# First layer's expert rows scattered to token order; the second convolution loads them plainly

## The reference

```
x = x + relu(segment_sum(Z[src] * edge_weight))         # Z = layernorm(x) @ W
x = x + ffn0(layernorm(x))      # attention (8 heads), then 64 experts, top 2
x = x + conv1(layernorm(x))     # mean of neighbours @ W_l.T + x @ W_r.T, relu, batch norm
x = x + ffn1(layernorm(x))      # 8 experts, top 2, hidden 256
```

```
pos  = place of the choice in its expert's queue        # cumulative count
keep = pos < C                                          # the rest is dropped
buf  = zeros(E, C, H).at[ef, posc].add(tok)             # 64 x 78 rows of 512
h    = gelu(buf @ w1[e] + b1[e]);  y = h @ w2[e] + b2[e]
out  = sum over the 2 choices of y[ef, posc] * (gate * keep)
```

## Time and profile before

| what | value |
|---|---|
| median of three runs | 1474.98 us (1473.58 to 1478.74) |
| the profiled execution: its own time | 1486.91 us |
| its span, first to last instruction | 1485.1 us |
| mean granted TensorE clock | 0.974 |
| TensorE matmuls busy | 1405.3 us, 95% |
| VectorE / ScalarE / GpSimd busy | 750.1 / 464.1 / 225.5 us |
| first experts, first turn to last output product | 782.61 to 1052.45 us |
| from there to the first neighbour sum | to 1103.65 us |
| DMA moved | 142.38 MB |

### The profile page before, as it was taken

The page is one execution under the profiler, slowest core; times in us unless marked ns, Lnnn a source line. Parts: engine busy times, 40 slices in busy tenths (PEclk is TensorE's granted clock), DMA queues, the critical chain, the costliest instruction groups (busy, mean ns, idle before and its releaser), DMA issues. The chain is left out here.

```text
span 1485.1 us, 24276 instructions
## 1 busy us (share of the span) xinstructions
PE 1405.3 (95%) x7939; PEld 904.7 (61%) x7940; DVE 750.1 (51%) x1591; ACT 464.1 (31%) x1153; POOL 225.5 (15%) x356
## 2 busy tenths in 40 slices
PE   8999999999999999999988999999899999889968
PEld 4688854455477777776556666666445555646632
DVE  7899956552278788875662222222250012544421
ACT  3599931111055555553021111111340011211111
POOL 1133310000000000000212222222420000012234
PEclk9999999999999999999998999999999999799988
DMA  5000000020000000001338999999420000823336
GB/s 153 29 0 0 0 0 0 0 85 0 28 2 2 1 2 1 2 1 48 113 72 271 322 332 322 328 323 324 138 60 0 0 0 0 301 53 128 127 95 171
DMA packets 94075, 142.38 MB, mean 96 GB/s; under 512 B 13301, under 2 KB 50571, under 8 KB 93879
## 3 DMA queue, kind: packets, MB, share of 16 engines
q1 hardware_dynamic: 69313, 97.52, 21.4%
q0 software_dynamic: 14976, 26.81, 6.5%
q10 hardware_dynamic: 9718, 17.12, 3.4%
HBM read 115.09 MB, written 26.29 MB: 95 GB/s over the span
## 5 line engine op out<-in xcount | busy, mean ns | idle before, releaser
L1240 PEld LDWEIGHTS ps<-b_r 128*128 128x128 f32 x1024 | 125.4, 193 | 34.3 <-issue 32.8
L1240 PE MATMUL ps<-b_r 128*128 128x78 f32 x1024 | 123.2, 274 | 1.1 <-DVE b_r L1302 1.1
L1249 PE MATMUL ps<-b_r 128*78 128x512 f32 x256 | 122.0, 600 | 0.0
L585 PE MATMUL ps<-b_r 125*125 125x160 f32 x660 | 118.3, 315 | 0.0
L500 ACT ACTIVATE b_r<-b_r 125x125 f32<-125x125 f32 x330 | 107.6, 389 | 9.2 <-DVE b_r L395 4.8
L1286 ACT ACTIVATE b_r<-ps,b_r 128x78 f32<-128x78 f32 x128 | 34.7, 323 | 230.5 <-PE ps L1240 226.7
L911 PEld LDWEIGHTS ps<-b_r 125*64 125x64 f32 x1600 | 85.3, 136 | 24.6 <-issue 22.8
L874 PE MATMUL ps<-b_r 64*125 64x417 f32 (+1 forms) x480 | 95.3, 529 | 1.4 <-DVE ps L1003 1.2
L911 PE MATMUL ps<-b_r 125*64 125x125 f32 x1600 | 94.7, 272 | 1.3 <-ACT b_r L939 1.3
L1144 POOL TENSOR_TENSOR b_x<-b_x,b_r 125x512 f32<-125x512 f32 x10 | 12.7, 1273 | 534.7 <-DVE b_r L1089 534.7
L1165 POOL DMA_INDIRECT b_r<-rows,b_ex_ids x88 | 85.7, 974 | 45.8 <-issue 40.7
(11 more groups left out here) (262 smaller groups left out, 2238.5 us busy)
## 6 DMA issues: line engine op xcount, KB each, us to landing
b_r<-L_ffn_w SPq DMA_DIRECT2D x128, 512.0 KB, 9.5
y<-b_r ACTq DMA_DIRECT2D x64, 156.0 KB
b_r<-L_ffn_W SPq DMA_DIRECT2D x2, 4096.0 KB, 20.5
y<-b_r ACTq DMA_DIRECT2D x24, 256.0 KB, 2.4
rows<-b_r SPq DMA_DIRECT2D x2, 2400.0 KB
b_x<-x SPq DMA_DIRECT2D x5, 480.0 KB
out<-b_x SPq DMA_DIRECT2D x10, 240.0 KB
y<-b_r SPq DMA_DIRECT2D x1, 2048.0 KB, 11.0
```

The source lines that it names most:

```text
L585: last = pe.matmul(T.ps[:P, 2 + b, 0:WC], T.weighted[:, b, j, :], T.cells[:, b, j, :], start=(j == 0), stop=(j == CJ - 1))
L1240: last = pe.matmul(T.ps[:, 2 + r % 2, f * CAP:(f + 1) * CAP], T.ew1[r % WS][:, k, f * 128:(f + 1) * 128], T.ex_t[:, r % 2, k, :], start=(k ...
L1249: last = pe.matmul(T.ps[:CAP, 4 + r % 2, :], T.eh[:, r % 2, f, :], T.ew2[r % WS][:, f, :], start=(f == 0), stop=(f == FK - 1))
```

## The change

1. `y0` has 2 * 1250 rows, in token order: row j * 1250 + token holds the expert output of choice j. In the attention block SyncE writes x into all of it once (4 DMAs, 5.1 MB), so that rows of dropped choices hold finite numbers.
2. The table gives 4128 for an empty place (iota with offsets, `EMPTY` added). A second table `sids` (10 more matmuls, `make_choices`, and two more VectorE operations) gives j * 1250 + token. Indirect DMAs get a bound and leave out indices beyond it; in the second layer's gathers too.
3. `first_experts`: 4 slots for gathered and for output rows; GpSimd issues the gathers straight from `ids` as written out, and the stores as indirect DMAs (scatters) six experts behind. ScalarE stores nothing.
4. After the last expert, in the same block: the 32 weight transposes and their copies, then the 10 products gates @ b2 with VectorE adding them to x; SyncE waits for the last scatter and loads `y0` with 20 plain DMAs (10 of 120 partitions and 2 tiles, 10 of 5 partitions), on one semaphore for each pair of tiles.
5. `second_convolution` has no gathers, no weight turns and no bias product; its filler matmuls stay.
6. `finish` waits on one semaphore for each pair of tiles (4 gathers) where it waited for 2 gathers of a tile. Several semaphores are shared; that changes no order.

```diff
 def token_ids(dve, link, T, bank, rows, columns):
-    link(dve.tensor_copy(T.ids_low[:rows, 0:columns], T.ps[:rows, bank, 0:columns]))
+    link(dve.tensor_scalar(T.ids_low[:rows, 0:columns], T.ps[:rows, bank, 0:columns], float(EMPTY), None, ALU.add))
     dve.scalar_tensor_tensor(out=T.ids[:rows, 0:columns], in0=T.ps[:rows, bank, columns:2 * columns], scalar=float(P),
                              in1=T.ids_low[:rows, 0:columns], op0=ALU.mult, op1=ALU.add)
+    link(dve.scalar_tensor_tensor(out=T.ids_low[:rows, 0:columns], in0=T.ps[:rows, bank, columns:2 * columns],
+                                  scalar=float(P), in1=T.ids_low[:rows, 0:columns], op0=ALU.mult, op1=ALU.add))
+def choice_ids(dve, T, bank, rows, columns):
+    return dve.scalar_tensor_tensor(out=T.sids[:rows, 0:columns], in0=T.ps[:rows, bank, 0:columns],
+                                    scalar=float(N), in1=T.ids_low[:rows, 0:columns], op0=ALU.mult, op1=ALU.add)
@@ attention, sync
+            for j in range(TOP):
+                for p0, p1 in ((0, 120), (120, P)):
+                    sp.dma_start(A.y0[j * N:(j + 1) * N].rearrange("(t p) d -> p t d", t=NT)[p0:p1], T.x[p0:p1])\
+                      .then_inc(S.rows_filled, 16)
+            sp.wait_ge(S.rows_filled, 80)
@@ gather_rows
         pool.indirect_dma_start(slots[:parts, r % 2, :], None, rows,
-                                bass.IndirectOffsetOnAxis(ap=T.ex_ids[:parts, r % 4:r % 4 + 1], axis=0))\
+                                bass.IndirectOffsetOnAxis(ap=T.ex_ids[:parts, r % 4:r % 4 + 1], axis=0),
+                                bounds_check=N - 1, oob_is_err=False)\
@@ first_experts
+    PEEL, SLOTS, LAG = 4, 4, 6
-            for slot in range(2):
+            for slot in range(SLOTS):
                 sp.wait_ge(S.ex_loaded[slot], 16)
             for slot in range(EARLY, WS):
                 load_expert(sp, T, S, A, slot, slot)
...
+            for slot in range(SLOTS):
+                sp.wait_ge(S.ey_stored[slot], 16 * E0 // SLOTS)
+            for i in range(NT // 2):
+                for p0, p1 in ((0, 120), (120, P)):
+                    for j, rows in enumerate((T.rows_a, T.rows_c)):
+                        sp.dma_start(rows[p0:p1, 2 * i:2 * i + 2],
+                                     A.y0[j * N:(j + 1) * N].rearrange("(t p) d -> p t d", t=NT)[p0:p1, 2 * i:2 * i + 2])\
+                          .then_inc(S.y_gathered[i], 16)
         def _(pool):
-            gather_rows(pool, T, A.rows0, T.ex, CAP, E0 // 4 - 2, S.ex_ids_ready, S.ex_turned, S.ex_loaded)
+            def gather(e):
+                if e >= SLOTS:
+                    pool.wait_ge(S.ex_turned, e - SLOTS + 1)
+                pool.indirect_dma_start(T.ex[:CAP, e % SLOTS, :], None, A.rows0,
+                                        bass.IndirectOffsetOnAxis(ap=T.ids[:CAP, e:e + 1], axis=0),
+                                        bounds_check=N - 1, oob_is_err=False).then_inc(S.ex_loaded[e % SLOTS], 16)
+            def scatter(e):
+                pool.wait_ge(S.ey_copied, e + 1)
+                pool.indirect_dma_start(A.y0, bass.IndirectOffsetOnAxis(ap=T.sids[:CAP, e:e + 1], axis=0),
+                                        T.ey[:CAP, e % SLOTS, :], None,
+                                        bounds_check=TOP * N - 1, oob_is_err=False).then_inc(S.ey_stored[e % SLOTS], 16)
+            for e in range(E0 + LAG):
+                if e < E0:
+                    gather(e)
+                if e == LAG:
+                    pool.wait_ge(S.rows_filled, 80)
+                if e >= LAG:
+                    scatter(e - LAG)
@@ tensor, after the last output product
+            for i, w in enumerate((T.w_a, T.w_b)):
+                for k in range(KD):
+                    bank = banks[KD * i + k]
+                    if bank >= 4 and i > 0:
+                        pe.wait_ge(S.ey_copied, E0)
+                    for m in range(KD):
+                        last = pe.transpose(T.ps[:, bank, m * 128:(m + 1) * 128], w[:, m, k * 128:(k + 1) * 128], T.ident[:])
+                    last.then_inc(S.wl_turned, 1)
+            pe.wait_ge(S.b2_loaded, 16)
+            pe.wait_ge(S.wl_copied, 2)
+            for t in range(NT):
+                if t >= 2:
+                    pe.wait_ge(S.bias_added, t - 1)
+                pe.matmul(T.ps[:P, 6 + t % 2, :], T.gates_t[:, t * P:(t + 1) * P], T.b2_rows, start=True, stop=True)\
+                  .then_inc(S.bias_done, 1)
@@ second_convolution, tensor
-            pe.wait_ge(S.wl_loaded, 32)
-            for i, w in enumerate((T.w_a, T.w_b)):
...
-            pe.wait_ge(S.wl_copied, 2 * KD)
-            pe.wait_ge(S.b2_loaded, 16)
...
-                pe.wait_ge(S.y_gathered[t], 32)
-                gated_sum(pe, T, t, t % 2, T.gates_t, T.b2_rows, rows).then_inc(S.moe_done, 1)
+                pe.wait_ge(S.y_gathered[t // 2], 64)
+                for j in range(TOP):
+                    last = pe.matmul(T.ps[:P, t % 2, :], T.diagonal[:, t % 2, j, :], rows[j][:, t, :],
+                                     start=(j == 0), stop=(j == TOP - 1))
@@ finish
-                pe.wait_ge(S.y_gathered[t], 64)
+                pe.wait_ge(S.y1_gathered[t // 2], 64)
```

More of the change, by code:

```diff
@@ L705, in make_table, with make_choices @@
     return last
+def make_choices(pe, T, bank, rows, place, columns):
+    for t in range(NT):
+        last = pe.matmul(T.ps[:rows, bank, 0:columns], T.place_rows[:, t * TOP + 1, :], place[:, 1, t, 0:columns],
+                         start=(t == 0), stop=(t == NT - 1))
+    return last
 def token_ids(dve, link, T, bank, rows, columns):
-    link(dve.tensor_copy(T.ids_low[:rows, 0:columns], T.ps[:rows, bank, 0:columns]))
+    link(dve.tensor_scalar(T.ids_low[:rows, 0:columns], T.ps[:rows, bank, 0:columns], float(EMPTY), None, ALU.add))
     dve.scalar_tensor_tensor(out=T.ids[:rows, 0:columns], in0=T.ps[:rows, bank, columns:2 * columns], scalar=float(P),
                              in1=T.ids_low[:rows, 0:columns], op0=ALU.mult, op1=ALU.add)
+    link(dve.scalar_tensor_tensor(out=T.ids_low[:rows, 0:columns], in0=T.ps[:rows, bank, columns:2 * columns],
[3 more added lines that the diff above has]
+                                    scalar=float(N), in1=T.ids_low[:rows, 0:columns], op0=ALU.mult, op1=ALU.add)
 def load_expert(sp, T, S, A, e, slot):
@@ L1185, in first_experts @@
     FK = F0 // 128
-    LOOPS = (E0 - 2) // WS
+    PEEL, SLOTS, LAG = 4, 4, 6
+    LOOPS = (E0 - PEEL) // WS
     def experts(engine, step):
-        for r in range(2):
+        for r in range(PEEL):
             step(0, r)
         with engine.Fori(0, LOOPS) as q:
-            for r in range(2, 2 + WS):
+            for r in range(PEEL, PEEL + WS):
                 step(q, r)
-        for r in range(2, 2 + (E0 - 2) % WS):
+        for r in range(PEEL, PEEL + (E0 - PEEL) % WS):
             step(LOOPS, r)
@@ L1267, in _ @@
             output(LOOPS, (E0 - 1) - WS * LOOPS)
+            banks = (6, 7, 0, 1, 2, 3, 4, 5)
+            pe.wait_ge(S.wl_loaded, 32)
+            pe.wait_ge(S.eh_ready, E0)
+            for i, w in enumerate((T.w_a, T.w_b)):
[8 more added lines that the diff above has]
+            pe.wait_ge(S.wl_copied, 2)
+            for t in range(NT):
+                if t >= 2:
+                    pe.wait_ge(S.bias_added, t - 1)
+                pe.matmul(T.ps[:P, 6 + t % 2, :], T.gates_t[:, t * P:(t + 1) * P], T.b2_rows, start=True, stop=True)\
+                  .then_inc(S.bias_done, 1)
         @block.scalar
@@ L1288, in step @@
                 last.then_inc(S.eh_ready, 1)
-                if not isinstance(q, int) or WS * q + r > 0:
-                    store(q, r - 1)
             experts(act, step)
-            store(LOOPS, (E0 - 1) - WS * LOOPS)
-            for slot in range(2):
-                act.wait_ge(S.ey_stored[slot], 8 * E0)
+            banks = (6, 7, 0, 1, 2, 3, 4, 5)
+            for i in range(2):
+                for k in range(KD):
+                    act.wait_ge(S.wl_turned, KD * i + k + 1)
+                    act.activation(T.wl_t[:, i, k, :], T.ps[:, banks[KD * i + k], :], ACT.Copy).then_inc(S.wl_copied, 1)
         @block.vector
@@ L1318, in _ @@
             output(LOOPS, (E0 - 1) - WS * LOOPS)
+            for t in range(NT):
+                dve.wait_ge(S.bias_done, t + 1)
+                dve.tensor_tensor(T.x[:, t, :], T.ps[:P, 6 + t % 2, :], T.x[:, t, :], ALU.add).then_inc(S.bias_added, 1)
 def second_convolution(nc, T, S, A):
@@ L1328, in second_convolution @@
     with nc.Block() as block:
[L1330 to L1336, removed]
         @block.tensor
@@ L1402, in counts @@
                 act.activation(T.ct_f[:, t], T.ct[:, t], ACT.Copy).then_inc(S.ct_ready, 1)
-            for i in range(2):
-                for k in range(KD):
-                    act.wait_ge(S.wl_turned, 4 * i + k + 1)
-                    act.activation(T.wl_t[:, i, k, :], T.ps[:, 4 * i + k, :], ACT.Copy).then_inc(S.wl_copied, 1)
             for t in range(2):
```

(1 more changed line is left out.)

94 lines of the change are left out of this document (46 added, 48 removed).

## The result

| | median us | runs | ratio to the kernel before, 95% |
|---|---|---|---|
| before | 1475.13 | 1473.58 to 1478.74 | |
| after | 1460.64 | 1455.69 to 1462.1 | 0.9891 [0.9864, 0.9919] |

The change gains 14.5 us in this comparison (medians of four runs each; the 1474.98 that the forecast starts from is the median of three); two later ones of the same two kernels gave 19.7 (ratio 0.987 [0.985, 0.9891]) and 19.1 us (0.9877 [0.9851, 0.9904]). Forecast were 22.8 us and 1452, with a range of 1444 to 1469. The profiled execution of the changed kernel took 1460.3 us, span 1458.5.

What follows compares the result with a forecast made beforehand. The expert stage was taken as bound by the latency of a two-deep gather, hardly by TensorE. Terms -4.9 - 17.4 - 1.5 + 1.0 = -22.8 us took the 1474.98 median to 1452.2, 1452 for short; range 1444 to 1469.

Steps and rivals of the forecast that it cites:

- The start (-4.9): First experts: four early gathers end TensorE's 2.9 us wait, output product at full clock takes 1.88 us: gain 4.9 us.
- The pace (-17.4): Expert stage, 63 remaining output products: 3.80 us each after, 4.08 before: gain 17.4 us (13.6 to 21.8).
- The sign that GpSimd's queue moves about 8 MB each way: Expert stage, expected in the profile after: GpSimd's queue at about 8 MB each way, DMA still at 300 GB/s or more.
- Why 4.0 before: Expert stage before: gather landing 6.8 us after issue, two slots, loop of 8.1 us for two steps, 4.05 each.
- Empty places: Rival, expert stage: empty places still cost a transfer, pace stays about 4.05 us, total 1467.9 us; chance 0.17.
- The seam (-1.5): Last output product to neighbour sums: first gated product 4.5 us later, ten tiles faster, sum -1.5 us (-4 to +6).
- The rival of the held SyncE: Seam: full queues hold SyncE's load issues, block ends 7.4 us later, total 1459.6 us; chance 0.13.
- finish (+1.0): Last block: tile 0 waits for four gathers, first product 2.8 us later; taken as +1.0 us (-1.5 to +3).
- The 4 us to be had back at tiles 8 and 9: End of finish: with a later start these tiles may avoid a wait and half clock, up to 4 us back.
- The base: Whole kernel: profiled execution 11.9 us above the median; difference carried over to the median, 1474.98 - 22.8 = 1452.2 us.
- GpSimd: Rival, expert steps: GpSimd becomes the bound; gain gone at 2.6 us a scatter, about 1532 us at 3.5; chance 0.08.

Runs made afterwards that it cites:

- the kernel with two lists: Changed kernel with 8 of the 20 loads left in SyncE's expert-stage list and 12 issued at the second convolution's start: 1452.63 us, ratio 0.9852.

## Why the prediction was right, and where it was off

Right in direction and place, and in half of the cause; 8.3 us too much in this comparison, 3 to 4 in the other two. By the means of three profiles each, the difference is 22.6 us: -0.8 to F, -24.9 in F to E, +1.3 in E to N, +0.8 in N to G, +1.0 behind it. That this meets the 22.8 of the forecast is luck: F to E gained 2.6 more than its two terms and E to N 2.8 less, and the three profiled executions of before (1480.8 in the mean) lie above its medians of 1475.1 to 1477.6. What the change is worth is the medians' 14.5 to 19.7.

- **The start (-4.9).** From F to the start of the third output product: 19.6, 17.3 and 19.4 us before, 15.9, 15.9 and 13.5 after, so -3.7 in the mean. The four early gathers did away with the wait of 2.9 us. The rest of the term was a product at the full clock, 1.88 us, and in two of three profiles it ran at the low level (3.57 and 3.52 us; in the first the granted clock is 0.66 over 785 to 790). In the third it took 1.88, and the gain was there.
- **The pace (-17.4).** Too cautious: 3.73 in all three profiles where I took 3.80. The mis-sized part is the price of a MB of weights. Over 800 to 1000 us their queue took 86.0% of 200 us for 56.55 MB, 3.04 us a MB or 3.19 an expert and not 3.42, and gathers and scatters 0.42. That is 3.61 us an expert, under TensorE's 3.73. Before, the same window has 3.24 us a MB (80.3% for 49.54 MB), and with all rows gathered 3.34: the price is higher where the share is above 1, so one read under overload was too dear for a kernel with fewer bytes. (The sign that GpSimd's queue moves about 8 MB each way was a slip: 64 times my 0.062 MB is 4 each way.) So the 61 steps gained 20 to 23 us.
- **Why 4.0 before.** I named the latency of a two-deep gather. That is half of it. With two slots and fewer bytes the pace is 3.75, with four slots and all bytes 3.73 until the stock of weights is gone. In these kernels the loop of two slots binds only where the DMA engines are overloaded: over 800 to 1000 us the share is 1.05 before and 1.06 with two slots and all rows, both with waits for gathers, and 0.94 with two slots alone, where one turn waits 0.5 us.
- **Empty places.** The rival fell. Gathering all rows put 6.27 MB back on GpSimd's queue (24.46 and not 18.19); 3068 empty places of 2 KB are 6.28. Its page has:

```profile
q0 software_dynamic: 14592, 24.46, 5.8%
```

- **The seam (-1.5).** This failed: +1.3 in the mean and +3.7 against the second profile of before. Three terms: SyncE's list took 13.25 us and not 8.8, ending 3.9 late; the fillers took 5.04 and not 4.1, as TensorE had idled 5.2 us first; the tiles and what follows them took 29.9 us and not 31.1. Of that, VectorE's first add to its last took 22.9 us (2.54 a tile in the mean; most steps are 2.39, three are 1.7, 3.0 and 3.8), as forecast with 2.5; but before it had taken 28.8 (3.2 a tile), not nine times 2.97, so the nine tiles saved 5.9 and not 4.2, and tile 0 saved 1.3 of its 1.8. The rival of the held SyncE was half right: the mechanism holds and was put at 0.13, with 3.9 of its 7.4 us. My argument against it, issues into empty queues, was true for the first fourteen loads only (0.30 to 0.45 us each; the last six take 0.38 to 2.23, 7.4 in all).
- **finish (+1.0).** As forecast in the main: the first product 2.3 us later behind G (2.8 foreseen), and two tiles at the low clock ahead of eight without a wait. The 4 us to be had back at tiles 8 and 9 were there in the first profile of before only; the other two have no such wait.
- **The base.** I carried 11.9 us of the profiled execution over to the median, and said that the gain shrinks by what of it is gather waiting: that was 5.3. With it the pace's gain is that of the typical execution, F to E 264.6 to 242.4, -22.2, where the two terms said -22.3. What is then missing of 22.8 is the seam, and some 2 to 3 us spread over stretches that the change doesn't touch (to F: 777.7 to 782.8 among all profiles; N to G: 330.9 to 335.4).
- **GpSimd.** Never near the bound: 1.02 and 0.97 us. Beside VectorE's copies 54 gathers took 1.01 to 1.03 us, so these runs again show no sign of the lock that the Trainium skill describes ("SBUF — State Buffer", section "Who interferes with whom"). Of the one queue for GpSimd that the Trainium skill states ("DMA: Bandwidth & Descriptors", section "SWDGE vs HWDGE vs iDMA") they show no price: scatters stand between all gathers, and with four slots no turn waits for one.

## What to carry to other kernels

A stage that waits for short transfers while long ones fill the DMA engines has two cures, fewer bytes and an earlier request. Try each alone before building both, because here each was worth most of the pair. Follow the stage to its end: with eight slots of weights a shortage of DMA needed 140 us to show. The new seam cost more than the old one, so plain loads in token order are no gain of their own here. And a list of loads at the end of a block belongs to that block's length, so leave there only what the next block needs first.

## What the runs showed of the hardware

The plain loads were dearer than expected. Windows of the kernel after, over the loads:

```profile
1027.00:1040.00 13.00, 8.40 (x18) 2.31 (x16) 6.88 (x10) 0.00 (x0) 0.00 (x0) 0.94 0.92 196
1040.00:1046.00 6.00, 5.38 (x14) 2.06 (x15) 0.00 (x0) 4.82 (x7) 0.00 (x0) 0.56 1.00 217
```

The DMA engines are as full as under the weights (318 GB/s at 0.97) and move 196 to 217 GB/s, 4.7 us of all engines a MB against 3.0. Single issues of SyncE took up to 2.2 us (median 0.38), all the long ones behind the fourteenth; in the kernel with two lists none of the 20 took over 0.49. That the issues were held because so much was still to be moved is my reading of these two. Why these loads are dearer, no run here tells. The size of a row alone does not explain it: the kernel before gathered the same rows of `y0` at 3.7 us a MB (5.14 MB, 40.8% of 47 us).

An empty place moves no bytes and still counts as packets: GpSimd's queue has 14592 of them in both kernels, with 18.19 and 24.46 MB. The difference in share is 21 us of all engines over 6.27 MB (4.4% of 1458.5 against 5.8% of 1467.2), 3.3 us a MB, where the whole queue has 3.5. By that gap all 3068 empty places together cost about 1 us of all engines, an estimate within the rounding of the two shares: next to nothing.
